# Row group 2 of the products on two banks in turn, the spread on the banks left idle, and bias matmuls with operands stored in pass order

## The chip, the cores and the metric

The kernel runs on one core of a Trainium2 chip. The metric is the device time of one execution in microseconds (us). The kernel before was timed three times, with a median of 274.6 us (274.46 to 275.27). One more execution was profiled, and all rows come from that one. The engines are called by the profile's names: PE is the matrix engine and PEld its weight loads, DVE the vector engine, ACT the activation engine, POOL the general engine, SP the one that issues most transfers.

## The reference, cut to what matters

```
r_goods (2048, 200, 32) fp32, r_candidate_ad (2048, 32) fp32
outer  = einsum('bi,bnj->bnij', candidate_ad, goods).reshape(B, N, 32*32)
h1     = concatenate((broadcast candidate_ad, goods, outer), axis=-1)
act    = sigmoid(h1 @ W1 + b1)          # W1: (32*34, 36), 36 hidden columns
weight = act @ W2 + b2
out    = sum(goods * weight, axis=1)    # (2048, 32)
```

For one batch row the outer product with the candidate can be folded into the weights, so that the first layer is a 32 by 36 matrix of its own for every batch row, and a bias that depends on the candidate.

## The kernel before

**Units and pairs.** A unit is 4 batch rows (one for each group r of 32 partitions), and 8 units make what the code calls a pair p; there are 64 pairs. A set-up stage makes the folded weights of all batch rows: `step` runs fp32 matmuls of 512 columns (line 295), ACT and DVE move them to `wm` and `wxd` (lines 481 and 525), two groups of bias matmuls follow (line 308 into `x_ps`, line 315 into `w_ps`), DVE copies the first four pairs' weights to `wm_ring` (line 537), and the first products start.

**One slot of PE.** In slot p PE executes, in this order, which is written out by hand: half 0 of the products of pair p (line 342, s = 0: for r in 0 to 3 and c in 0 to 3 one 32 by 32 matmul of 200 columns; the trace shows two weight loads and two matmuls for each), the spread of pair p-3, f = 0 (line 426, four bf16 matmuls of 64 by 128), half 1 of the products (s = 1), the spread f = 1, the row sums of pair p-1 (line 387, 12 matmuls of 128 by 32 into `w_ps`), and the x products of pair p (line 363, 8 matmuls of 128 by 32 into `x_ps`, the four hidden columns over 32). The first four slots (`FILL`) are unrolled and the rest is a loop of ten turns of six slots. In slots 0 to 2 there is no spread.

**The other engines.** For a pair, ACT makes eight activates of 200 columns (line 502, r = 0 to 3, s = 0 and 1), one for x (line 508) and one copy to the weight ring (line 489). Its activate of r needs `z_done` of r, which the last matmul of r in half 1 raises. After the second activate of r = 2 it raises `z_read`. DVE then pools: `pool_units` multiplies the spread row sums with the goods and adds them up, 8 instructions a pair, each with a read of the accumulator behind it (line 556), and `keep` takes the row sums out of `w_ps` (lines 544 and 546). POOL splits these into three bf16 parts (lines 263, 265 and 271), which the spread three slots later sums again. SP issues the goods of pair p, four transfers of 200 KB, during slot p-3.

**Banks.** There are eight PSUM banks: `z_ps` 0 to 3, `x_ps`, `w_ps`, `s_ps[0]`, `s_ps[1]`. Products r = 0, 1, 2 always write `z_ps` 0, 1, 2, and r = 3 writes `z_ps` 3 and `s_ps[0]` in turn. The spread writes `w_ps` and `s_ps[1]` (f = 0), and `x_ps` and the bank that r = 3 of the pair before used (f = 1).

**Waits of PE around the change.** Before half 0: `goods_loaded`, `z_read` of the pair before (line 336) and `pooled[1][1]` (line 339). Before the spread f = 0: `w_kept`, `pooled[0][1]` (line 401) and `stack_made`; f = 1: `actx_done`. Before the row sums: `pooled[0][0]`. Before the x products: `pooled[1][0]` (line 359, in every third slot with `wx_laid` besides). `pooled[f][s]` is raised by DVE after the second instruction on bank s of spread f.
Of the kernel before, what the change touches and what calls it, by code (L numbers as in the profile page):

```python
# [7 lines left out]
ALU = mybir.AluOpType  # L8
ACT = mybir.ActivationFunctionType

P = 128
# [36 lines left out]

def build(nc, goods_t, cand_r, cand_u, w1_outer, small, pick, out_t):
    with ExitStack() as ctx:  # L50
# [6 lines left out]
        def sem(name):  # L57
            return ctx.enter_context(nc.semaphore(name))
# [22 lines left out]
        early = act[:, :, :, :].rearrange("p a r n -> p (a r n)")  # L81
        cand = early[:, 0:4 * UNITS].rearrange("p (r u) -> p r u", r=4)
        candu = early[:, 4 * UNITS:5 * UNITS]
        w1 = early[:, 5 * UNITS:5 * UNITS + (T_MAIN + 1) * K].rearrange("p (t j) -> p t j", j=K)
# [20 lines left out]
        def z_bank(p, r):  # L105

            return z_ps[:, r, :] if r < 3 else (z_ps[:, 3, :], s_ps[0][:, :])[p % 2]

        def s_banks(q, f):

            if q + LAG >= PAIRS:

                z0, z1, z2, z3 = (z_ps[:, r, :] for r in range(4))
                return (((z0, z1), (z2, z3)), ((s_ps[1], x_ps), (z0, z1)), ((z2, z3), (s_ps[1], x_ps)))[q + LAG - PAIRS][f]

            return ((w_ps, s_ps[1]), (x_ps, z_bank(q + LAG - 1, 3)))[f]

# [24 lines left out]
        cand_loaded = sem("cand_loaded")  # L143
        candu_loaded = sem("candu_loaded")
        w1_loaded = sem("w1_loaded")
        pick_loaded = sem("pick_loaded")
# [11 lines left out]
        x_done = sem("x_done")  # L158
        z_read = sem("z_read")
        actx_done = sem("actx_done")  # L160
        w_done = sem("w_done")
# [26 lines left out]
        def _(sp):  # L188
            sp.dma_start(cand[:, :, :], cand_r[:, :, :]).then_inc(cand_loaded, 16)

            sp.wait_ge(cand_loaded, 16)
            sp.dma_start(candu[:, :], cand_u[:, :]).then_inc(candu_loaded, 16)
            sp.dma_start(pick_sb[:, :, :], pick[:, :, :]).then_inc(pick_loaded, 16)
            sp.wait_ge(w1_loaded, 16)
            sp.wait_ge(consts_loaded, 16)
            def in_iteration(i, j):

                if j == 0:
                    sp.wait_ge(actx_done, i)
                if j == 1:  # L200
                    sp.wait_ge(z_done, 4 * i + 1)
                if j == 2:
                    sp.wait_ge(z_done, 4 * i + 4)
                if j == 3:
                    sp.wait_ge(z_read, i + 1)

# [75 lines left out]
        def _(pe):  # L282
# [21 lines left out]
            pe.wait_ge(wb_kept[1], kept(T_MAIN - 1, 1))  # L304
            pe.wait_ge(consts_loaded, 16)
            for c in range(4):
                src = cand[0:K, :, :].rearrange("i r (p s c) -> i c r p s", s=2, c=4)
                last = nc.tensor.matmul(x_ps[32 * c:32 * c + 32, :], w1c[0:K, :], src[:, c],  # L308
                                        start=True, stop=True)
            last.then_inc(bias_made, 1)  # L310
            pe.wait_ge(candu_loaded, 16)
            for s in range(2):
                for c in range(4):
                    src = candu[:, :].rearrange("i (p s c) -> i s c p", s=2, c=4)
                    last = nc.tensor.matmul(w_ps[32 * c:32 * c + 32, 0:PAIRS], w1x[:, s, :], src[:, s, c],
                                            start=s == 0, stop=s == 1)
# [7 lines left out]
            def products(p, slot, s, loaded=None):  # L324

                pe.wait_ge(pick_loaded, 16)
                if s == 0:

                    pe.wait_ge(goods_loaded[slot % G_SLOTS], loaded)  # L330
                    if slot < FILL:
                        pe.wait_ge(ring_filled, slot + 1)
                    if slot >= 1:

                        pe.wait_ge(z_read, p)
                    if slot >= LAG + 1:

                        pe.wait_ge(pooled[1][1], p)
                for r in range(4):  # L340
                    for c in range(4):
                        last = nc.tensor.matmul(z_bank(slot, r)[32 * c:32 * c + 32, N * s:N * s + N],  # L342
                                                wm_ring[32 * r:32 * r + 32, slot % RING, 4 * s + c, :],
                                                goods[32 * r:32 * r + 32, slot % G_SLOTS, 4 * s + c, :],
                                                start=True, stop=True)
                    if s == 1:
                        last.then_inc(z_done, 1)
# [43 lines left out]
            def spread(p, slot, f):  # L391

                q = slot - LAG
                if f == 0:
                    pe.wait_ge(stack_made, p)
                    if slot < PAIRS:

                        pe.wait_ge(w_kept, p)
                    if 1 <= q and slot < PAIRS:

                        pe.wait_ge(pooled[0][1], p)
                    if slot == PAIRS:

                        pe.wait_ge(z_read, p)
                    if slot == PAIRS + 1:

                        pe.wait_ge(pooled[0][1], p - 1)
                    if slot == PAIRS + 2:
# [3 lines left out]
                else:  # L412
# [3 lines left out]
                    if slot == PAIRS:  # L416

                        pe.wait_ge(pooled[1][1], p)
                    if slot > PAIRS:
# [48 lines left out]
        def _(sc):  # L468
# [26 lines left out]
            for p in range(PAIRS):  # L495
# [3 lines left out]
                for r in range(4):  # L499
                    sc.wait_ge(z_done, 4 * p + r + 1)  # L500
                    for s in range(2):
                        last = nc.scalar.activation(act[:, p % A_SLOTS, r, N * s:N * s + N],  # L502
                                                    z_bank(p, r)[:, N * s:N * s + N], ACT.Sigmoid,
                                                    bias=bias[:, r, p, s:s + 1])
                    if r == 2:
                        last.then_inc(z_read, 1)
                sc.wait_ge(x_done, p + 1)
# [7 lines left out]
        def _(dve):  # L515
# [31 lines left out]

            def pool_units(q, f, amid=None):
                dve.wait_ge(s_done, 2 * q + f + 1)
                for s in range(2):  # L550
                    if s == 1 and amid is not None:
                        keep(amid)
                    for i in range(2):
                        v = 4 * s + 2 * f + i
                        u = PAIR_U * q + v
                        last = nc.vector.tensor_tensor_reduce(  # L556
                            goods[:, q % G_SLOTS, v, :], s_banks(q, f)[s][:, N * i:N * i + N], goods[:, q % G_SLOTS, v, :],
                            1.0, 0.0, ALU.mult, ALU.add, out_stage[:, u:u + 1])

                    last.then_inc(pooled[f][s], POOLED_FROM[f][s] + 1 if q == 0 else 1)  # L560

            for p in range(PAIRS + LAG):
                q = p - LAG
                if q >= 0:
                    pool_units(q, 0)

                    pool_units(q, 1, PAIRS - 1 if p == PAIRS else None)
                if 1 <= p < PAIRS:
                    keep(p - 1)
# [64 lines left out]
```

## Time and profile before

| what | value |
|---|---|
| three timed runs | 274.46, 274.60, 275.27 us (median 274.6) |
| the profiled execution | 274.75 us, of which the span is 273.0 us |
| mean granted clock of PE | 0.992 of full speed |
| PE, PEld | busy 95% and 47% of the span |
| DVE, ACT, POOL | busy 76%, 82%, 54% |
| chain that ended last | PE 89%, ACT 3%, DVE 3% |
| read from HBM | 54.19 MB, 199 GB/s over the span |

The span runs from the first to the last instruction in the trace; the 1.75 us around it belong to the execution but to none of its instructions. The busy share of PE counts a matmul until the end that the profile models for it, and matmuls overlap, so 95% doesn't mean that nothing more fits. In a timeline, a row gives start and length of a group of like instructions that follow each other; in brackets is the idle time of the engine before it and what ended it.

### The profile page before, as it was taken

How to read it: one execution, taken by the hardware profiler on the slowest of the kernel's cores; microseconds unless marked ns; L12 is line 12 of the kernel's file. 1: busy time of each engine (PE TensorE's matmuls, PEld its weight loads, DVE VectorE, ACT ScalarE, POOL GpSimd, SP SyncE). 2: the span in 40 equal slices, each digit the busy share in tenths (PEclk: the TensorE clock that was granted, in tenths of full speed). 3: DMA queues.
4: the chain of work that ended last, by engine and by line, in shares of the span. 5: the costliest groups of instructions: out<-in, count | busy, mean ns of one | idle time of the engine just before them, and what ended most of it. 6: DMA issues, size and time to landing. Idle time of an engine off the chain costs nothing.

```text
span 273.0 us, 18351 instructions
## 1 busy us (share of the span) xinstructions
PE 258.4 (95%) x7492; PEld 127.4 (47%) x7492; DVE 208.0 (76%) x1176; ACT 223.2 (82%) x658; POOL 146.7 (54%) x285
## 2 busy tenths in 40 slices
PE   8997999999999999999999999999999999999980
PEld 2324544444454544555445554454544445445540
DVE  0892567877778777787777877778777787777886
ACT  2998878888898888988889888898888988889850
POOL 1300664565555755557555575555665556655562
PEclk9999999999999999999999999999999999999996
DMA  5872766767776777776787777777777776776100
GB/s 200 254 289 62 224 208 186 226 210 232 223 214 213 215 227 228 217 208 204 229 232 214 216 206 226 224 223 214 202 221 233 217 208 206 231 235 209 39 1 10
DMA packets 38195, 54.84 MB, mean 201 GB/s; under 512 B 4240, under 2 KB 37904, under 8 KB 38032
## 3 DMA queue, kind: packets, MB, share of 16 engines
q1 hardware_dynamic: 37872, 54.15, 66.3%
q10 hardware_dynamic: 288, 0.32, 0.3%
q8 instruction: 11, 0.18, 0.3%
q14 instruction: 24, 0.20, 0.2%
HBM read 54.19 MB, written 0.26 MB: 199 GB/s over the span
## 4 chain that ended last, share of the span: by engine, by line
PE 89%; ACT 3%; DVE 3%; DMA 2%; issue 2%; DVEq 0%
PE z_ps L342 27%; PE w_ps L387 25%; PE x_ps L363 18%; PE w_ps L426 6%; PE x_ps L426 6%; ACT act L502 3%; PE z_ps L295 3%; DVE goods L556 2%; DMA act<-w_outer 2%; PE s_ps L342 1%; PE s_ps L295 1%; PE x_ps L295 1%; PE x_ps L308 1%; PE w_ps L295 0%; PE s_ps L426 0%
## 5 line engine op out<-in xcount | busy, mean ns | idle before, releaser
L502 ACT ACTIVATE act<-z_ps,bias 128x200 f32<-128x200 f32 x448 | 149.4, 439 | 34.2 <-PE z_ps L342 17.7
L342 PE MATMUL z_ps<-goods,wm_ring 32*32 32x200 f32 x3584 | 79.6, 339 | 5.7 <-ACT act L502 1.9
L556 DVE CUSTOM_DVE_ANT_0 goods<-w_ps,goods 128x200 f32<-128x200 f32 x122 | 39.8, 364 | 45.2 <-PE s_ps L426 45.2
L263 POOL TENSOR_TENSOR rest<-whole,top 128x200 f32<-128x200 f32 x64 | 36.1, 565 | 66.7 <-DVE top L546 36.7
L556 DVE CUSTOM_DVE_ANT_0 goods<-s_ps,goods 128x200 f32<-128x200 f32 x186 | 60.1, 361 | 0.0
L363 PE MATMUL x_ps<-goods,wx 128*32 128x200 f32 x1024 | 56.7, 338 | 0.2
L387 PE MATMUL w_ps<-act,consts 128*32 128x200 f32 x1024 | 56.6, 339 | 0.3 <-ACT actx L508 0.3
L265 POOL TENSOR_SCALAR mid<-rest,consts 128x200 bf16<-128x200 f32 x64 | 50.1, 783 | 6.3
L342 PEld LDWEIGHTS z_ps<-goods,wm_ring 32*32 32x32 f32 x3584 | 32.1, 103 | 39.3 <-issue 38.6
L241 POOL COPY wx<-wxd 32x96 f32<-32x96 f32 (+1 forms) x88 | 22.9, 260 | 42.3 <-PE x_ps L363 28.1
L556 DVE DVE_READ_ACCUMULATOR2_ANT out_stage<- 128x1 f32 x512 | 42.5, 83 | 0.0
L556 DVE CUSTOM_DVE_ANT_0 goods<-x_ps,goods 128x200 f32<-128x200 f32 x126 | 40.8, 361 | 0.0
L363 PEld LDWEIGHTS x_ps<-goods,wx 128*32 128x32 f32 x1024 | 28.6, 109 | 24.6 <-DVE out_stage L556 12.3
L271 POOL TENSOR_TENSOR stack<-rest,mid 128x200 bf16<-128x200 f32 x64 | 36.3, 567 | 5.4
L342 PE MATMUL s_ps<-goods,wm_ring 32*32 32x200 f32 x512 | 34.7, 340 | 0.0
L387 PEld LDWEIGHTS w_ps<-act,consts 128*32 128x32 f32 x1024 | 26.8, 109 | 16.1 <-DVE out_stage L556 10.0
L387 PE MATMUL w_ps<-actx,consts 128*32 128x200 f32 x512 | 33.4, 333 | 0.0
L544 DVE TENSOR_SCALAR whole<-w_ps,consts 128x200 f32<-128x200 f32 x64 | 27.0, 422 | 7.6 <-PE w_ps L387 7.6
L426 PE MATMUL s_ps<-stack,pick_sb 64*128 64x200 bf16 x186 | 31.9, 252 | 0.5 <-POOL stack L271 0.5
L508 ACT ACTIVATE actx<-x_ps,biasx 128x200 f32<-128x200 f32 x64 | 30.6, 478 | 0.0
L489 ACT ACTIVATE wm_ring<-wm 128x256 f32<-128x256 f32 x60 | 28.9, 482 | 0.0
L502 ACT ACTIVATE act<-s_ps,bias 128x200 f32<-128x200 f32 x64 | 24.9, 466 | 0.0
(45 smaller groups left out, 225.5 us busy)
## 6 DMA issues: line engine op xcount, KB each, us to landing
goods<-goods_t SPq DMA_DIRECT2D x256, 200.0 KB, 2.8
act<-cand_r SPq DMA_DIRECT2D x1, 1024.0 KB, 5.3
act<-cand_u SPq DMA_DIRECT2D x1, 256.0 KB, 2.7
out_t<-out_stage SPq DMA_DIRECT2D x4, 64.0 KB, 2.6
consts<-small ACTq DMA_DIRECT2D x1, 164.5 KB, 5.3
act<-w_outer ACTq DMA_DIRECT2D x1, 144.0 KB, 5.5
pick_sb<-pick SPq DMA_DIRECT2D x1, 128.0 KB, 2.6
```

The costliest lines, as they stand in the source:

```text
L263: nc.gpsimd.tensor_tensor(rest[:, :], whole[:, q % 2, :], top[:, q % 2, :], ALU.subtract).then_inc(part_step, 1)
L265: nc.gpsimd.tensor_scalar(mid[:, :], rest[:, :], m2, None, ALU.mult).then_inc(part_step, 1)
L271: nc.gpsimd.tensor_tensor(stack[:, q % 2, :], rest[:, :], mid[:, :], ALU.subtract).then_inc(stack_made, STACK_FROM + 1 if q == 0 else 1)
L342: last = nc.tensor.matmul(z_bank(slot, r)[32 * c:32 * c + 32, N * s:N * s + N], wm_ring[32 * r:32 * r + 32, slot % RING, 4 * s + c, :], go ...
L363: last = nc.tensor.matmul(x_ps[32 * c:32 * c + 32, 0:N], left, goods[:, slot % G_SLOTS, 4 * s + c, :], start=s == 0, stop=s == 1)
L387: last = nc.tensor.matmul(w_ps[32 * t:32 * t + 32, 0:N], left, right, start=step == 0, stop=step == 2)
L426: last = nc.tensor.matmul(s_banks(q, f)[s][:, N * i:N * i + N], pick_sb[rows, 2 * f + i, :], stack[rows, q % 2, :], start=True, stop=True)
L489: nc.scalar.activation(*of_ring(p), ACT.Identity)
L502: last = nc.scalar.activation(act[:, p % A_SLOTS, r, N * s:N * s + N], z_bank(p, r)[:, N * s:N * s + N], ACT.Sigmoid, bias=bias[:, r, p, s ...
L508: nc.scalar.activation(actx[:, p % A_SLOTS, :], x_ps[:, 0:N], ACT.Sigmoid, bias=biasx[:, p:p + 1]).then_inc(actx_done, 1)
L544: nc.vector.tensor_scalar(whole[:, p % 2, :], w_ps[:, 0:N], b2, None, ALU.add).then_inc(w_kept, KEPT_FROM + 1 if p == 0 else 1)
L556: last = nc.vector.tensor_tensor_reduce(goods[:, q % G_SLOTS, v, :], s_banks(q, f)[s][:, N * i:N * i + N], goods[:, q % G_SLOTS, v, :], 1. ...
```

## The change

Row group 2 of the products now alternates as row group 3 does: r = 2 writes `z_ps` 2 or `s_ps[0]`, r = 3 writes `z_ps` 3 or `s_ps[1]`. The spread f = 0 writes `w_ps` and the bank that r = 2 of the pair before used, f = 1 writes `x_ps` and that of r = 3. ACT raises `z_read` after r = 1 and a new `z2_read` after r = 2; half 0 waits for the first, the spread f = 0 for the second. The wait for `pooled[1][1]` moves from before half 0 to between r = 1 and r = 2 of half 0, and `pooled[0][1]` moves there from the spread. DVE pools in another order: the second unit of f = 0 on the z bank comes after the two units of `x_ps`, so that `x_ps` is free after five units instead of six. In the set-up the operands of the bias matmuls come from a new array `candb` (its own transfer on SP's queue, between those of `candu` and `pick_sb`) and a reordered `candu`, so that PE reads neighbouring elements. The order of PE's matmuls and their number stay.

```
 def z_bank(p, r):
-    return z_ps[:, r, :] if r < 3 else (z_ps[:, 3, :], s_ps[0][:, :])[p % 2]
+    return z_ps[:, r, :] if r < 2 or p % 2 == 0 else s_ps[r - 2][:, :]
 def s_banks(q, f):
     if q + LAG >= PAIRS:
         z0, z1, z2, z3 = (z_ps[:, r, :] for r in range(4))
-        return (((z0, z1), (z2, z3)), ((s_ps[1], x_ps), (z0, z1)), ((z2, z3), (s_ps[1], x_ps)))[q + LAG - PAIRS][f]
-    return ((w_ps, s_ps[1]), (x_ps, z_bank(q + LAG - 1, 3)))[f]
+        return (((z0, z1), (z2, z3)), ((s_ps[0], s_ps[1]), (z0, z1)), ((z2, z3), (s_ps[0], s_ps[1])))[q + LAG - PAIRS][f]
+    return ((w_ps, x_ps)[f], z_bank(q + LAG - 1, 2 + f))
...
 @block.sync
             sp.dma_start(candu[:, :], cand_u[:, :]).then_inc(candu_loaded, 16)
+            sp.dma_start(candb[:, :, :], cand_b[:, :, :]).then_inc(candb_loaded, 16)
             sp.dma_start(pick_sb[:, :, :], pick[:, :, :]).then_inc(pick_loaded, 16)
...
                 if j == 3:
-                    sp.wait_ge(z_read, i + 1)
+                    sp.wait_ge(z2_read, i + 1)
...
+            pe.wait_ge(candb_loaded, 16)
             for c in range(4):
-                src = cand[0:K, :, :].rearrange("i r (p s c) -> i c r p s", s=2, c=4)
-                last = nc.tensor.matmul(x_ps[32 * c:32 * c + 32, :], w1c[0:K, :], src[:, c],
+                last = nc.tensor.matmul(x_ps[32 * c:32 * c + 32, :], w1c[0:K, :], candb[:, c, :],
...
-                    src = candu[:, :].rearrange("i (p s c) -> i s c p", s=2, c=4)
+                    src = candu[:, :].rearrange("i (s c p) -> i s c p", s=2, c=4)
...
 def products(p, slot, s, loaded=None):
                         pe.wait_ge(z_read, p)
-                    if slot >= LAG + 1:
+                for r in range(4):
+                    if s == 0 and r == 2 and slot >= LAG + 1:
+                        pe.wait_ge(pick_loaded, 16)
+                        pe.wait_ge(pooled[0][1], p)
                         pe.wait_ge(pooled[1][1], p)
-                for r in range(4):
                     for c in range(4):
...
 def spread(p, slot, f):
                         pe.wait_ge(w_kept, p)
-                    if 1 <= q and slot < PAIRS:
-                        pe.wait_ge(pooled[0][1], p)
+                        pe.wait_ge(z2_read, p)
...
                     if slot == PAIRS:
+                        pe.wait_ge(pooled[0][1], p)
                         pe.wait_ge(pooled[1][1], p)
...
 @block.scalar
+                    if r == 1:
+                        last.then_inc(z_read, 1)
                     if r == 2:
-                        last.then_inc(z_read, 1)
+                        last.then_inc(z2_read, 1)
...
 @block.vector
-                    pool_units(q, 0)
-                    pool_units(q, 1, PAIRS - 1 if p == PAIRS else None)
+                    dve.wait_ge(s_done, 2 * q + 1)
+                    pool_unit(q, 0, 0, 0)
+                    pool_unit(q, 0, 0, 1)
+                    pool_unit(q, 0, 1, 0)
+                    if p >= PAIRS:
+                        pool_unit(q, 0, 1, 1)
+                    dve.wait_ge(s_done, 2 * q + 2)
+                    pool_unit(q, 1, 0, 0)
+                    pool_unit(q, 1, 0, 1)
+                    if p < PAIRS:
+                        pool_unit(q, 0, 1, 1)
+                    if p == PAIRS:
+                        keep(PAIRS - 1)
+                    pool_unit(q, 1, 1, 0)
+                    pool_unit(q, 1, 1, 1)
```

`pool_unit(q, f, s, i)` is the body of the old inner loop, one instruction; it raises `pooled[f][s]` where i is 1.

## Rows read from the trace of the kernel before

**Rows 1.** The page: busy time by engine (part 1), and transfers (part 6).
```profile
PE 258.4 (95%) x7492; PEld 127.4 (47%) x7492; DVE 208.0 (76%) x1176; ACT 223.2 (82%) x658; POOL 146.7 (54%) x285
...
goods<-goods_t SPq DMA_DIRECT2D x256, 200.0 KB, 2.8
```

**Rows 2.** Timeline of PE's weight loads, one slot: start, length, line, groups.
```profile
145.34 0.22 PEld L342 LDWEIGHTS z_ps<-goods,wm_ring 32*32 32x32 f32 x21 [0.44 <-issue]
...
145.93 0.09 PEld L426 LDWEIGHTS w_ps<-stack,pick_sb 64*128 64x128 bf16 x1 [0.32 <-issue]
...
146.21 0.18 PEld L342 LDWEIGHTS z_ps<-goods,wm_ring 32*32 32x32 f32 x20 [0.16 <-issue]
...
146.76 0.09 PEld L426 LDWEIGHTS x_ps<-stack,pick_sb 64*128 64x128 bf16 x1 [0.32 <-issue]
...
147.04 0.50 PEld L387 LDWEIGHTS w_ps<-act,consts 128*32 128x32 f32 x16 [0.16 <-DVE out_stage L556]
...
149.12 0.29 PEld L342 LDWEIGHTS z_ps<-goods,wm_ring 32*32 32x32 f32 x23 [0.35 <-issue]
```

**Rows 3.** Timeline of PE's matmuls, the same slot.
```profile
145.46 0.37 PE L342 MATMUL s_ps<-goods,wm_ring 32*32 32x200 f32 x4
...
146.03 0.25 PE L426 MATMUL s_ps<-stack,pick_sb 64*128 64x200 bf16 x1
...
146.48 0.35 PE L342 MATMUL s_ps<-goods,wm_ring 32*32 32x200 f32 x4
...
148.28 0.89 PE L363 MATMUL x_ps<-goods,wx 128*32 128x200 f32 x16
```

**Rows 4.** Timeline of ACT: the slot before, and this one.
```profile
143.10 2.65 ACT L502 ACTIVATE act<-z_ps,bias 128x200 f32<-128x200 f32 x8 [0.49 <-PE z_ps L342]
...
145.90 0.48 ACT L489 ACTIVATE wm_ring<-wm 128x256 f32<-128x256 f32 x1
146.88 2.01 ACT L502 ACTIVATE act<-z_ps,bias 128x200 f32<-128x200 f32 x6 [0.49 <-PE s_ps L342]
```

**Rows 5.** Timeline of DVE, the same slot.
```profile
146.32 0.37 DVE L556 CUSTOM_DVE_ANT_0 goods<-w_ps,goods 128x200 f32<-128x200 f32 x1 [0.70 <-PE s_ps L426]
...
148.04 0.08 DVE L556 DVE_READ_ACCUMULATOR2_ANT out_stage<- 128x1 f32 x1
...
148.62 0.08 DVE L556 DVE_READ_ACCUMULATOR2_ANT out_stage<- 128x1 f32 x1
```

**Rows 6.** Source view of line 339, 148.5 to 149.3: duration ns, first and last start.
```profile
L339 PEldq EVENT_SEMAPHORE  x1: 51/51/51, 149.0 to 149.0; - x1
```

**Rows 7.** Weight loads and matmuls of slot 1, and starts of slots 3, 63.
```profile
23.73 0.22 PEld L342 LDWEIGHTS z_ps<-goods,wm_ring 32*32 32x32 f32 x21 [1.62 <-issue]
...
24.99 0.50 PEld L387 LDWEIGHTS w_ps<-act,consts 128*32 128x32 f32 x16 [0.32 <-issue]
...
25.87 0.64 PEld L363 LDWEIGHTS x_ps<-goods,wx 128*32 128x32 f32 x16
...
26.03 0.86 PE L363 MATMUL x_ps<-goods,wx 128*32 128x200 f32 x16
...
30.33 0.22 PEld L342 LDWEIGHTS z_ps<-goods,wm_ring 32*32 32x32 f32 x21 [0.52 <-issue]
...
259.12 0.22 PEld L342 LDWEIGHTS z_ps<-goods,wm_ring 32*32 32x32 f32 x21 [0.44 <-issue]
```

**Rows 8.** Source view of line 332 (a wait behind slot 1's x products), 25 to 26.
```profile
L332 PEldq EVENT_SEMAPHORE  x1: 51/51/51, 25.7 to 25.7; - x1
```

**Rows 9.** The set-up: groups by line (busy us, mean ns), then two timeline rows.
```profile
L295 PE MATMUL z_ps<-act 32*32 32x512 f32 x160 | 9.2, 600 | 0.1
...
L308 PE MATMUL x_ps<-act,consts 32*32 32x512 f32 x8 | 2.0, 1066 | 0.0
...
19.67 0.50 DVE L537 COPY wm_ring<-wm 128x256 f32<-128x256 f32 x2
...
20.37 0.93 PEld L342 LDWEIGHTS z_ps<-goods,wm_ring 32*32 32x32 f32 x64 [0.21 <-issue]
```

More of the change, by code:

```diff
@@ L46, with build @@
 C_ALL = C_M2 + 1
-def build(nc, goods_t, cand_r, cand_u, w1_outer, small, pick, out_t):
+def build(nc, goods_t, cand_r, cand_b, cand_u, w1_outer, small, pick, out_t):
     with ExitStack() as ctx:
@@ L82, in build @@
         cand = early[:, 0:4 * UNITS].rearrange("p (r u) -> p r u", r=4)
+        candb = sb("candb", [K, 4, 4 * 2 * PAIRS])
         candu = early[:, 4 * UNITS:5 * UNITS]
@@ L144, in build @@
         candu_loaded = sem("candu_loaded")
+        candb_loaded = sem("candb_loaded")
         w1_loaded = sem("w1_loaded")
@@ L159, in build @@
         z_read = sem("z_read")
+        z2_read = sem("z2_read")
         actx_done = sem("actx_done")
@@ L398, in spread @@
                         pe.wait_ge(w_kept, p)
-                    if 1 <= q and slot < PAIRS:
-                        pe.wait_ge(pooled[0][1], p)
+                        pe.wait_ge(z2_read, p)
                     if slot == PAIRS:
                         pe.wait_ge(z_read, p)
-                    if slot == PAIRS + 1:
-                        pe.wait_ge(pooled[0][1], p - 1)
                     if slot == PAIRS + 2:
@@ L546, in keep, with pool_unit @@
                 nc.vector.tensor_scalar(top[:, p % 2, :], whole[:, p % 2, :], m1, None, ALU.mult).then_inc(top_made, 1)
[L548 to L560, printed above, removed]
+            def pool_unit(q, f, s, i):
+                v = 4 * s + 2 * f + i
+                u = PAIR_U * q + v
+                one = nc.vector.tensor_tensor_reduce(
+                    goods[:, q % G_SLOTS, v, :], s_banks(q, f)[s][:, N * i:N * i + N], goods[:, q % G_SLOTS, v, :],
+                    1.0, 0.0, ALU.mult, ALU.add, out_stage[:, u:u + 1])
+                if i == 1:
+                    one.then_inc(pooled[f][s], POOLED_FROM[f][s] + 1 if q == 0 else 1)
             for p in range(PAIRS + LAG):
@@ L586 @@
     by_unit = np.asarray(r_candidate_ad).reshape(UNITS, 4, K).transpose(1, 2, 0)
-    cand_u = np.ascontiguousarray(by_unit).reshape(P, UNITS)
+    by_pair = by_unit.reshape(4, K, PAIRS, 2, 4)
+    cand_u = np.ascontiguousarray(by_pair.transpose(0, 1, 3, 4, 2)).reshape(P, UNITS)
+    cand_b = np.ascontiguousarray(by_pair.transpose(1, 4, 0, 2, 3)).reshape(K, 4, 4 * 2 * PAIRS)
     cand_r = np.ascontiguousarray(np.tile(by_unit.transpose(1, 0, 2), (4, 1, 1)))
@@ L624 @@
     arrays, args = {}, []
-    for name, a in (("goods_t", goods_t), ("cand_r", cand_r), ("cand_u", cand_u), ("w1_outer", w1_outer),
+    for name, a in (("goods_t", goods_t), ("cand_r", cand_r), ("cand_b", cand_b), ("cand_u", cand_u), ("w1_outer", w1_outer),
                     ("small", small), ("pick", pick.reshape(P, 4, P))):
```

## The prediction, made before the changed kernel was run

> **What bounds the kernel now.** I read the page first. PE is busy 95% of the span, ACT 82%, DVE 76% [rows 1], and the chain of waits runs through PE nearly all the way. That says only that PE has hardly any empty moment, not that its work sets the pace, since a matmul counts until its modelled end. So I went to the timelines of one slot in mid-loop and asked, for each start on PE, what it could have started at.
>
> The slot runs from 145.34 to 149.12, a period of 3.78 us [rows 2]. Inside it each change of tile form starts its first weight load 0.07 before the modelled end of the last matmul ahead of it: the spread's matmul ends at 146.28 and half 1 loads at 146.21; the last group of half 1 ends at 146.83 and the spread loads at 146.76 [rows 2, 3]. I take this 0.07 as the mark of a start that waits for PE alone. At the end of the slot the mark is missed, though barely: the x products end at 148.28 + 0.89 = 149.17 and the next half 0 loads at 149.12. More telling is slot 1, where nothing makes the x products wait: they load 0.88 after the row sums' first load (24.99, 25.87) and end 1.90 after it (26.89) [rows 7]. With the mark, the next half 0 could load 1.90 - 0.07 = 1.83 after the row sums' first load. In the loop it is 149.12 - 147.04 = 2.08 [rows 2]. So 0.25 us of each slot is not PE's work.
>
> Two waits share it. The first is a closed loop with ACT. Half 0 loads at 145.34, ACT's first activate starts at 146.88 (1.54 later), its sixth, the second of r = 2, ends at 148.89 (2.01 later) [rows 4], and half 0 of the next slot loads at 149.12 (0.23 later, in which PE's sequencer executes two waits; the second, of 51 ns, starts at 149.0, about 0.1 ahead of the load [rows 2, 6]). 1.54 + 2.01 + 0.23 = 3.78, the whole period, so this loop sets the pace. The second is DVE: the sixth accumulator read, which frees `x_ps`, ends at 148.12 [rows 5], against a load that PE could make at 147.04 + 0.88 = 147.92. Removing only one of the two would leave most of the time where it is.
>
> **The change, part by part.** *z_read after r = 1.* The activates start 0.31 apart (eight take 2.65, the last 0.47 of it) [rows 4], so the signal comes 0.62 earlier and the loop needs 1.54 + 1.39 + 0.23 = 3.16 us. It no longer binds.
>
> *DVE's order.* `x_ps` is free after the fifth unit. Units are 0.29 apart (148.62 - 148.04 for two), so it ends at 148.12 - 0.29 = 147.83 [rows 5]. A signal takes some 0.04 (DVE starts at 146.32 behind the spread's end at 146.28 [rows 3, 5]); with 0.06 for signal and load I get 147.89, in time for 147.92. Where a second wait stands before it, in every third slot, it is some 0.04 late, but in slot 1 the matmul starts 0.16 behind its load (26.03 against 25.87) [rows 7], which covers that. The fourth unit now needs the spread f = 1, which ends at 147.04 + 0.07 = 147.11, so DVE could start it at 147.15; its turn comes at 146.32 + 3 x 0.29 = 147.19. No stall, with 0.04 to spare.
>
> Here a rule of the Trainium skill speaks against the gain. The page "TensorE: Matmul & The Clock Gate", section "Part 3: Packing small matmuls — row/col tiling", says that a weight load overlaps matmuls in flight only if it is for another row group. Loads of x and row sums use all rows, so by it an early signal would buy nothing. Slot 1 shows the x loads beginning at 25.87 while row-sum matmuls are in flight, so I go by the row and keep the rule as a rival.
>
> *The wait inside half 0.* This is what the change adds, and the trace of before has no such wait. Behind it in PE's order stand the loads of r = 2 and 3, and behind these the spread and everything else. The semaphores themselves are early: the eighth read ends at 148.70, about 148.74 at PE, and half 0 would start at 145.34 + 3.54 = 148.88 at the earliest. What remains is the sequencer's time. Below: nothing, if it executes the wait ahead of the array. It can do so, since the wait behind slot 1's x products starts at 25.7 and the first of these loads at 25.87 [rows 7, 8]. Above: the whole 0.23 from signal to load. r = 3 starts its matmuls 0.12 after half 0's first load [rows 2, 3], so r = 2 starts near 0.05; if the wait is executed only with the first loads, r = 2 comes near 0.10. I take 0.05. In exchange half 0 loses one of the two waits ahead of it. Half 0 lasts 0.59 and half 1, which has no wait of its own, 0.55 [rows 2], so the new half 0 is 0.55 + 0.05 = 0.60 (0.55 to 0.78).
>
> *z2_read before the spread f = 0.* It comes at 148.89, needed at 148.88 + 0.60. Hidden by half 0, 0.55 to spare.
>
> *The sum for a slot.* Half 0 0.60, spread 0.28, half 1 0.55, spread 0.28 [rows 2], row sums to the next load 1.83: 3.54 instead of 3.78, 0.24 less.
>
> *Who else must keep up.* ACT's ten instructions take 143.10 to 146.38, 3.28 [rows 4]; DVE is busy 76% of the time, 2.9 of a slot, and POOL 54% [rows 1]. All are under 3.54. Goods are issued three slots ahead and land in 2.8 us [rows 1], against 10.6. DVE's new order delays the second of a pair's four transfers by two units, 0.58, and the two behind it on SP's queue follow; three slots hide that.
>
> *Set-up.* Reading 512 neighbouring columns takes 600 ns a matmul and the strided bias matmuls 1066 [rows 9]; the second set of four starts behind the first, so some 0.9 us go. The path gets less, since DVE's copy to the ring is next: of two that take 0.50 together the first starts at 19.67 and ends, by my estimate, at 19.96, and with 0.12 for signal, wait and load the products start at 20.08 instead of 20.37 [rows 9]. 0.29 less. The new transfer is 64 KB beside goods of 200 KB each. Its issue stands ahead of the goods on SP's queue; slot 0 waits for the ring copy, so I take nothing for it.
>
> *Slots 0 to 3.* The wait of 1.62 before slot 1 [rows 7] is on z_read: 0.62 less. Slots 1 and 2 have no spread and need 24.99 - 23.73 + 1.83 = 3.09 each; now they take (30.33 - 23.73) / 2 = 3.30. 0.42 less. But the row sums of slot 1 then wait for ACT's x activate, by my estimate 0.27: that activate moves up by 0.29 only, PE by 0.91. Together 0.62 + 0.42 - 0.27 + 0.29 = 1.06.
>
> *Total.* From slot 3 (30.33) to slot 63 (259.12) there are 60 periods [rows 7], and slot 63 itself: 61 x 0.24 = 14.6. With 1.06 it is 15.7. The tail behind, DVE's, keeps its order and its length. The profiled execution took 274.75, so 259.05; the median of the runs is 0.15 lower. I say 259.0 us.
>
> **The rivals.** *The sequencer can't look past the wait* (row groups 2 and 3 start 0.2 late, half 0 0.75, period 3.69): 61 x 0.09 + 1.06 = 6.6, so 268. For it: two waits and a load do cost 0.23 today. Against: rows 8.
>
> *The x products gain nothing from DVE's order*, the skill's rule above, as a mechanism here: they load at 148.12 + 0.06 = 148.18, 1.14 after the row sums, and take 0.89, so the next half 0 loads 1.96 after these instead of 1.83. The period is 3.67, 61 x 0.11 + 1.06 = 7.8, so 267. Slot 1 speaks against it.
>
> *Another loop holds the slot near 3.78*, for instance goods that come late, and the change does nothing in the loop: only 1.06 goes, 273.7. No row has PE waiting for goods.
>
> *Slower*: the wait empties the array, and r = 2 and 3 run behind r = 0 and 1 in full. A half's matmul row has 0.35 to 0.37 [rows 3], about 0.33 of it new time, so half 0 becomes 0.93 and the period 3.87: 61 x 0.09 - 1.06 = 4.4 more, 279. It decides from a half 0 above 0.86, that is when the wait costs over 0.3.
>
> **How the numbers follow.** Forecast 0.68, sequencer 0.13, x products 0.08, nothing in the loop 0.05, slower 0.04, the rest 0.02 unnamed. A measurement of this kernel tells 0.3%, 0.8 us, from no change. Faster by more: 0.68 + 0.13 + 0.08 and most of the 0.05 (273.7 is just past the bound), 0.92; the same 0.03; slower 0.05. The forecast's own range is a period of 3.50 to 3.60, 256.9 to 262.7. The range given reaches to the x products' case and to the sequencer's, whose cost isn't known: 257 to 268.5.
>
> **What would show it.** Period 3.54; half 0 about 0.60 and r = 2's matmuls 0.10 behind its start; every change of tile form, that into half 0 too, 0.07 before the end ahead of it; x loads 0.88 behind the row sums; ACT idle some 0.25 a slot. The first products near 20.1, slot 3 near 29.3. I am wrong if half 0 is long, or if x still follows DVE at 1.14.

## The result, and the profile after

The changed kernel takes 262.6 us, the median of four runs (262.55 to 263.06). The kernel before, run in turn with it, took 274.9 us (274.46 to 275.62). The ratio is 0.9554, with a 95% interval of 0.9528 to 0.9579: 4.5% faster. The forecast was 259.0 us with a range of 257.0 to 268.5. The direction and the route were right, and 3.5 us of the forecast gain of 15.7 did not come. The profiled execution took 262.6 us with a span of 260.8, against 273.0 before: 12.2 us less.

The page of the changed kernel: busy time by engine, the x products' loads with the idle time ahead of them, and the new transfer (KB, us from issue to landing).

```profile
PE 248.3 (95%) x7492; PEld 133.6 (51%) x7492; DVE 209.6 (80%) x1176; ACT 224.3 (86%) x658; POOL 147.0 (56%) x285
...
L370 PEld LDWEIGHTS x_ps<-goods,wx 128*32 128x32 f32 x1024 | 33.0, 109 | 10.6 <-issue 0.3
...
candb<-cand_b SPq DMA_DIRECT2D x1, 256.0 KB, 3.8
```

PE is busy 95% before and after [rows 1], though the span is 12.2 us shorter: its busy time fell by 10.1 us with the same 7492 matmuls, since more of them overlap. So the share doesn't tell the room that is left. The x products now load with 10.6 us of idle time ahead of 1024 loads, and what ended most of it is no longer DVE. The transfer for `candb` is 256 KB. The prediction called it 64 KB; it hides either way, since the loads of the bias matmuls wait 0.4 us for ACT's `wm` in both kernels and not for it.

The timeline of PE's weight loads in one slot, which answers to [rows 2]: start, length, groups.

```profile
139.75 0.18 PEld L349 LDWEIGHTS z_ps<-goods,wm_ring 32*32 32x32 f32 x16 [0.32 <-issue]
139.85 0.21 PEld L349 LDWEIGHTS s_ps<-goods,wm_ring 32*32 32x32 f32 x16
140.38 0.09 PEld L430 LDWEIGHTS w_ps<-stack,pick_sb 64*128 64x128 bf16 x1 [0.32 <-issue]
...
140.66 0.15 PEld L349 LDWEIGHTS z_ps<-goods,wm_ring 32*32 32x32 f32 x12 [0.16 <-issue]
...
141.21 0.09 PEld L430 LDWEIGHTS x_ps<-stack,pick_sb 64*128 64x128 bf16 x1 [0.32 <-issue]
...
141.49 0.50 PEld L394 LDWEIGHTS w_ps<-act,consts 128*32 128x32 f32 x16 [0.16 <-DVE out_stage L557]
...
142.41 0.59 PEld L370 LDWEIGHTS x_ps<-goods,wx 128*32 128x32 f32 x16
143.33 0.31 PEld L349 LDWEIGHTS z_ps<-goods,wm_ring 32*32 32x32 f32 x32 [0.32 <-issue]
```

The slot lasts 143.33 - 139.75 = 3.58 (3.572 is the median over the loop from slot 16 on), where 3.54 was forecast. Half 0 takes 0.63, the spread 0.28, half 1 0.55, the spread 0.28, and the row sums to the next load 1.84. PE's matmuls in the same slot (timeline):

```profile
142.19 0.52 PE L394 MATMUL w_ps<-actx,consts 128*32 128x200 f32 x8
142.53 0.87 PE L370 MATMUL x_ps<-goods,wx 128*32 128x200 f32 x16
```

The x products end at 142.53 + 0.87 = 143.40, and the next half 0 loads at 143.33, 0.07 ahead: the mark of a start that waits for PE alone is now met at the end of the slot too. ACT, in the timeline of the same slot, has slack where it had set the pace:

```profile
141.33 1.38 ACT L506 ACTIVATE act<-z_ps,bias 128x200 f32<-128x200 f32 x4 [0.27 <-PE s_ps L349]
```

Its idle time was forecast at some 0.25 a slot.

**Where the time went.** I took the start of half 0 in every slot of both profiled executions and split the span at four of them. The rows of after that carry this (PE's weight loads; the rows of before are in [rows 7], except slot 10, which started at 58.12):

```profile
20.12 1.04 PEld L349 LDWEIGHTS z_ps<-goods,wm_ring 32*32 32x32 f32 x64 [0.88 <-ACT wm L485]
...
29.30 0.15 PEld L349 LDWEIGHTS z_ps<-goods,wm_ring 32*32 32x32 f32 x12 [0.32 <-issue]
...
57.56 0.24 PEld L349 LDWEIGHTS z_ps<-goods,wm_ring 32*32 32x32 f32 x20 [0.32 <-issue]
...
246.93 0.18 PEld L349 LDWEIGHTS z_ps<-goods,wm_ring 32*32 32x32 f32 x16 [0.32 <-issue]
```

| stretch | before | after | gained | forecast |
|---|---|---|---|---|
| start to slot 3 | 30.33 | 29.30 | 1.03 | 1.06 |
| slots 3 to 10 (7 slots, the loop's first turn and a slot) | 27.79 | 28.26 | -0.47 | 7 x 0.24 = 1.7 |
| slots 10 to 63 (53 slots) | 201.00 | 189.37 | 11.63 | 53 x 0.24 = 12.7 |
| slot 63 to the end | 13.84 | 13.88 | -0.04 | 0.24 |
| span | 273.0 | 260.8 | 12.2 | 15.7 |

So 3.5 us are short, and the largest part, 2.2, is in seven slots at the beginning. The prediction had no line for them. That 2.2 is one execution against one: the changed kernel profiled again (e11 below) took 28.95 for the seven, which would make it 2.8.

### The profile page after: what moved, and what is told of

It is laid out like the page before. It is cut to its first block, busy times and chain, and to the rows that moved or that the text cites. A ratio compares the mean times of both kernels' runs of the same rounds, so it can differ in the third digit from the quotient of the medians.

```text
span 260.8 us, 18353 instructions
## 1 busy us (share of the span) xinstructions
PE 248.3 (95%) x7492; PEld 133.6 (51%) x7492; DVE 209.6 (80%) x1176; ACT 224.3 (86%) x658; POOL 147.0 (56%) x285
## 4 chain that ended last, share of the span: by engine, by line
PE 87%; ACT 7%; DVE 2%; DMA 2%; issue 1%; ACTq 0%; DVEq 0%
PE w_ps L394 28%; PE z_ps L349 25%; PE x_ps L370 16%; PE w_ps L430 6%; PE x_ps L430 6%; PE s_ps L349 4%; ACT wm L485 4%; DMA act<-w_outer 2%; DVE goods L557 2%; ACT act L506 2%; ACT wxd L485 1%; PE z_ps L300 0%; ACT actx L514 0%; DVE whole L550 0%; PE z_ps L430 0%
## 5 line engine op out<-in xcount | busy, mean ns | idle before, releaser
L506 ACT ACTIVATE act<-z_ps,bias 128x200 f32<-128x200 f32 x384 | 129.4, 440 | 20.5 <-PE z_ps L349 10.9
L370 PE MATMUL x_ps<-goods,wx 128*32 128x200 f32 x1024 | 55.4, 333 | 0.0
L349 PEld LDWEIGHTS z_ps<-goods,wm_ring 32*32 32x32 f32 x3072 | 30.3, 103 | 34.4 <-issue 33.0
L557 DVE CUSTOM_DVE_ANT_0 goods<-z_ps,goods 128x200 f32<-128x200 f32 x140 | 44.9, 361 | 0.0
L506 ACT ACTIVATE act<-s_ps,bias 128x200 f32<-128x200 f32 x128 | 44.9, 461 | 0.0
L557 DVE CUSTOM_DVE_ANT_0 goods<-s_ps,goods 128x200 f32<-128x200 f32 x128 | 41.3, 361 | 0.0
L557 DVE CUSTOM_DVE_ANT_0 goods<-x_ps,goods 128x200 f32<-128x200 f32 x122 | 39.5, 361 | 1.3 <-PE s_ps L430 1.0
L370 PEld LDWEIGHTS x_ps<-goods,wx 128*32 128x32 f32 x1024 | 33.0, 109 | 10.6 <-issue 0.3
L349 PE MATMUL s_ps<-goods,wm_ring 32*32 32x200 f32 x1024 | 37.0, 339 | 0.0
```

Of the source, the lines that this page charges most:

```text
L370: last = nc.tensor.matmul(x_ps[32 * c:32 * c + 32, 0:N], left, goods[:, slot % G_SLOTS, 4 * s + c, :], start=s == 0, stop=s == 1)
L557: one = nc.vector.tensor_tensor_reduce(goods[:, q % G_SLOTS, v, :], s_banks(q, f)[s][:, N * i:N * i + N], goods[:, q % G_SLOTS, v, :], 1.0 ...
```

## Experiments

The question was twofold: which of the two waits carried the gain, and where the missing 3.5 us are. All times stand beside runs of the kernel before on the same chip, whose medians were 274.8 to 275.1 us. The line numbers in a row are those of the kernel it comes from.

### The banks without DVE's order, DVE's order without the banks

**e1**: the changed kernel with DVE's order of units as it was.

```diff
...
-                    pool_unit(q, 0, 1, 0)
...
-                    dve.wait_ge(s_done, 2 * q + 2)
-                    pool_unit(q, 1, 0, 0)
-                    pool_unit(q, 1, 0, 1)
-                    if p < PAIRS:
-                        pool_unit(q, 0, 1, 1)
...
+                    pool_units(q, 0)
+                    pool_units(q, 1, PAIRS - 1 if p == PAIRS else None)
```

> The changed kernel with DVE's old order of units, so that x_ps is free after the sixth unit again. If the x products follow DVE as before, they load about 1.14 us after the row sums in two slots of three and 1.2 in the third, the slot becomes 3.70 to 3.79 us (mean near 3.73) instead of 3.57, and the time rises by some 8 to 9 us, to 271. If DVE's order was worth nothing (weight loads that use the same row groups can't overlap the row sums anyway), the slot stays at 3.57 and the time at 262.6.

Measured: 271.2 us (270.2 to 271.5), ratio 0.9866 [0.9846, 0.9886]. PE's weight loads in one slot of it:

```profile
140.62 0.50 PEld L394 LDWEIGHTS w_ps<-act,consts 128*32 128x32 f32 x16 [0.16 <-DVE out_stage L562]
...
141.77 0.50 PEld L370 LDWEIGHTS x_ps<-goods,wx 128*32 128x32 f32 x16 [0.31 <-DVE out_stage L562]
142.59 0.18 PEld L349 LDWEIGHTS z_ps<-goods,wm_ring 32*32 32x32 f32 x16 [0.32 <-issue]
```

The x products load 1.15 behind the row sums and wait for DVE. The next half 0 follows 1.97 behind the row sums, as the second rival had worked out (1.96). Its slot is 3.70 with half 0 at 0.63, and 3.79 in every third slot, where two waits stand ahead of the x products: 3.73 in the mean.

**e2**: the kernel before, with only DVE's new order.

```diff
-                    pool_units(q, 0)
-                    pool_units(q, 1, PAIRS - 1 if p == PAIRS else None)
...
+                    pool_unit(q, 0, 1, 0)
...
+                    dve.wait_ge(s_done, 2 * q + 2)
+                    pool_unit(q, 1, 0, 0)
+                    pool_unit(q, 1, 0, 1)
+                    if p < PAIRS:
+                        pool_unit(q, 0, 1, 1)
...
```

> The kernel before with DVE's new order alone. If the loop over ACT (products, activates up to r = 2, z_read, products) sets the pace, the slot stays at 3.78 us and the time at 274.9, though the x products now load 0.88 us behind the row sums. If PE's work from the row sums on was the pace, the slot falls by about 0.12 and the time to 267.

Measured: 275.2 us (274.2 to 276.0), ratio 1.0002 [0.9984, 1.0020]. PE's weight loads:

```profile
139.98 0.50 PEld L387 LDWEIGHTS w_ps<-act,consts 128*32 128x32 f32 x16 [0.16 <-DVE out_stage L551]
...
140.85 0.64 PEld L363 LDWEIGHTS x_ps<-goods,wx 128*32 128x32 f32 x16
142.06 0.27 PEld L342 LDWEIGHTS z_ps<-goods,wm_ring 32*32 32x32 f32 x32 [0.56 <-issue]
```

The x products load 0.87 behind the row sums, as forecast, and nothing comes of it. The idle time ahead of half 0 grows to 0.56 from 0.35 in [rows 2], and the slot stays at 3.78. The stall only moved, to the wait for `z_read`. Together the two runs show what the prediction had read from the timelines. The loop with ACT set the pace, DVE's order was the next bound, and each alone hides the other. DVE's order by itself is worth nothing, the rest of the change without it 274.9 - 271.2 = 3.7 us, and both together 12. The 3.7 are not the banks alone. e1 keeps the new set-up, the earlier slot 1 and the wait inside half 0; its slot 3 starts at 29.38, 0.95 sooner than before, and its slots 10 to 63 take 3.73 against 3.79.

### The set-up alone

**e3**: the kernel before, with `candb` and the reordered `candu`.

```diff
+            sp.dma_start(candb[:, :, :], cand_b[:, :, :]).then_inc(candb_loaded, 16)
...
-                last = nc.tensor.matmul(x_ps[32 * c:32 * c + 32, :], w1c[0:K, :], src[:, c],
+                last = nc.tensor.matmul(x_ps[32 * c:32 * c + 32, :], w1c[0:K, :], candb[:, c, :],
```

> The kernel before with the set-up's part alone: the bias matmuls read candb and the reordered candu. The bias matmuls take about 0.9 us less, but the first products wait for DVE's copy to the ring next, so they start 0.25 us sooner (20.1 instead of 20.4) and the time falls by 0.25 to 0.3 us, to 274.6. If nothing else stood behind them, it would fall by 0.9.

Measured: 274.3 us (273.9 to 275.5), ratio 0.9981 [0.9963, 0.9999]. The bias matmuls in the view by line (busy us, mean ns), and DVE's copy to the ring and the first products' loads in the timeline:

```profile
L311 PE MATMUL x_ps<-candb,consts 32*32 32x512 f32 x8 | 1.1, 600 | 0.0
```

```profile
20.05 0.50 DVE L540 COPY wm_ring<-wm 128x256 f32<-128x256 f32 x2
...
20.46 0.49 PEld L345 LDWEIGHTS z_ps<-goods,wm_ring 32*32 32x32 f32 x34 [0.90 <-ACT wm L484]
```

A matmul takes 600 ns in place of 1066, as the other 512-column matmuls do in [rows 9]. Of the time, up to 1 us fits the interval, and so does nearly nothing. In this execution the first products did not even start earlier (20.46 against 20.37), and among the profiled executions of kernels that share this set-up the start lay between 19.94 and 20.52. That spread comes from upstream, since the copy itself started between 19.53 and 20.11. Counted from the copy's start, the first products load 0.41 later here and 0.40 or 0.41 in all ten profiles that share this set-up, against 0.70 before [rows 9] and 0.77 in e2. So the path did get 0.29 shorter, and the copy is what PE waits for now.

### The wait inside half 0

The forecast gave 0.05 to the wait between r = 1 and r = 2. The changed kernel's chain of waits shows it, with the pieces of half 0 first and those of half 1 behind the spread (start, length):

```profile
139.82 0.33 PE z_ps L349 x8
140.15 0.12 PE s_ps L349 x7
140.28 0.05 PE z_ps L349 x7
140.32 0.13 PE s_ps L349 x8
...
140.73 0.33 PE z_ps L349 x8
141.06 0.05 PE s_ps L349 x8
141.11 0.12 PE z_ps L349 x8
```

In half 1 the second piece takes 0.05, in half 0 it takes 0.12: r = 2 and 3 come 0.07 later. The wait is executed only with the half's first loads (source view of its line; half 0 loads at 139.75 and 143.33, and in the trace the wait starts 0.023 behind these):

```profile
L347 PEldq EVENT_SEMAPHORE  x2: 51/51/51, 139.8 to 143.3; - x2
```

**e4**: both waits ahead of half 0, everything else as changed. **e10** is the same kernel again with more rounds, and **e11** the changed kernel again beside it.

```diff
-                for r in range(4):
-                    if s == 0 and r == 2 and slot >= LAG + 1:
-
-                        pe.wait_ge(pick_loaded, 16)
+                    if slot >= LAG + 1:
                         pe.wait_ge(pooled[0][1], p)
                         pe.wait_ge(pooled[1][1], p)
+                for r in range(4):
```

> The changed kernel with both pooled waits before half 0 instead of inside it. If the wait inside costs the 0.075 us by which half 0 (0.63) exceeds half 1 (0.55), half 0 becomes 0.55 to 0.59, the slot 3.50 to 3.54, and the time falls by 2 to 4 us, to 259 or 260.5. If the waits ahead of half 0 now hold it up (pooled[1][1] comes about 0.15 us before PE is free), the slot stays near 3.57 or grows and the time stays at 262.6 or above.

> The version with both pooled waits before half 0 once more, with more rounds, beside the changed kernel on one chip. 260.5, 2 us below the changed kernel, with the slot at 3.51 from slot 10 on and the first turn again held by code loading: slots 3 to 9 in 28 to 29.5 us, about what the slower kernels take for them.

> The changed kernel again, on the chip of the run before it: 262.6, slot 3.57, slots 3 to 9 in 27.5 to 28.5 us.

Measured: e4 260.5 us (260.0 to 261.6), ratio 0.9477 [0.9446, 0.9509]; e10 260.0 us (259.6 to 260.5), ratio 0.9443 [0.9428, 0.9458]; e11 263.2 us (261.8 to 263.9), ratio 0.9555 [0.9529, 0.9580]. The intervals of e10 and e11 don't overlap: the waits ahead of half 0 are 3.1 us better, 1.2%. PE's weight loads in e10:

```profile
142.73 0.25 PEld L347 LDWEIGHTS z_ps<-goods,wm_ring 32*32 32x32 f32 x32 [0.32 <-issue]
143.29 0.09 PEld L428 LDWEIGHTS w_ps<-stack,pick_sb 64*128 64x128 bf16 x1 [0.32 <-issue]
...
146.24 0.15 PEld L347 LDWEIGHTS z_ps<-goods,wm_ring 32*32 32x32 f32 x12 [0.32 <-issue]
```

Half 0 is 0.56 here (0.567 in the loop, against 0.630 in the changed kernel) and the slot 3.51. The wait inside half 0, which the change brings on top of the banks, costs 0.063 a slot and buys next to nothing: ahead of half 0 the two signals are already there in nearly every slot. Six of the 53 slots of e10 from slot 10 on took 3.54 to 3.64, so in the mean the slot is 0.05 shorter.

**e6**: the changed kernel with two more waits at that place, on semaphores met long before. A stand-alone wait instruction holds two semaphores, so this is one more instruction of the sequencer.

```diff
                     if s == 0 and r == 2 and slot >= LAG + 1:
                         pe.wait_ge(pick_loaded, 16)
+                        pe.wait_ge(candb_loaded, 16)
+                        pe.wait_ge(candu_loaded, 16)
                         pe.wait_ge(pooled[0][1], p)
```

> The changed kernel with two more waits inside half 0, on transfers that landed long ago, which make one more instruction for PE's sequencer. If what half 0 lost is sequencer time, each such instruction costs about 0.1 us there: half 0 0.73, slot 3.67, time 268 to 269. If the sequencer runs ahead of the array, nothing changes: 262.6.

Measured: 268.4 us (267.8 to 269.5), ratio 0.9766 [0.9732, 0.9799]. PE's weight loads, and then the source view of the two wait instructions:

```profile
141.91 0.18 PEld L351 LDWEIGHTS z_ps<-goods,wm_ring 32*32 32x32 f32 x16 [0.32 <-issue]
142.12 0.21 PEld L351 LDWEIGHTS s_ps<-goods,wm_ring 32*32 32x32 f32 x16
142.65 0.09 PEld L432 LDWEIGHTS w_ps<-stack,pick_sb 64*128 64x128 bf16 x1 [0.32 <-issue]
```

```profile
L348 PEldq EVENT_SEMAPHORE  x2: 51/51/51, 141.9 to 145.6; - x2
...
L349 PEldq EVENT_SEMAPHORE  x2: 51/51/51, 142.0 to 145.7; - x2
```

Row groups 2 and 3 now load 0.21 behind the start, against 0.10 in the changed kernel. Half 0 is 0.74 and the slot 3.685. So it is the instruction that costs, not the signal. The first costs 0.063 (half 0 0.567 without, 0.630 with), of which, as I read it, a part lies beside the loads of r = 0 and 1 (that part was not tried by itself). The next costs 0.11 (3.685 - 3.572), all of it on the path; the two instructions start 0.11 apart in the trace.

### The first turn of PE's loop

The seven slots from 3 on, one by one (from start of half 0 to the next):

| slot | 3 | 4 | 5 | 6 | 7 | 8 | 9 |
|---|---|---|---|---|---|---|---|
| before | 3.78 | 3.78 | 4.73 | 4.18 | 3.78 | 3.78 | 3.78 |
| changed | 3.51 | 3.85 | 4.66 | 3.96 | 3.58 | 4.71 | 3.99 |

Before, slots 5 and 6 were long. They still are, and 8 and 9 are long now too. The chain of waits of the changed kernel in slot 5:

```profile
36.73 0.49 PE z_ps L349 x14
37.23 0.53 issue
37.75 0.35 PE z_ps L349
```

PE stops in the middle of a half, between two products that wait for no engine. One suspect is the loading of its own code, since the loop's instructions are all new in its first turn. The transfers view has a queue of kind "instruction", q8, that moves 16 KB pieces. In the changed kernel it is there from 29.3 to 57.6 and gone from 58 to 246:

```profile
q8 instruction: 7, 0.11, 1.9%
```

**e7**: the first turn unrolled and the loop left with nine turns. The instructions executed stay the same, but six slots more run on code of their own.

```diff
+FLAT = FILL + RING
...
-            for p in range(FILL):
-                products(p, p, 0, 64)
+            for p in range(FLAT):
+                products(p, p, 0, 64 * (1 + p // G_SLOTS))
...
-            with pe.Fori(0, TURNS):
+            with pe.Fori(0, TURNS - 1):
```

> The changed kernel with one turn of PE's loop (six slots) written out ahead of the loop, which runs nine turns; the work is the same. If the slots of the first turn are held by the loading of PE's code (mean 4.1 us instead of 3.57 over slots 4 to 9), six more slots pay it: 2 to 3 us more, 265, with irregular slots up to slot 16. If something of the start of the kernel holds them (the goods' first transfers), the time stays at 262.6 and the slots are regular from slot 10.

Measured: 267.1 us (264.2 to 267.7), ratio 0.9675 [0.9614, 0.9736], 4.5 us more than the changed kernel. The four runs differ more than usual, and the profiled one is the slowest, so the figures of its slots are at the upper end. Slots 10 to 15, regular at 3.57 in the changed kernel, took 4.03, 6.02, 3.81, 3.63, 4.09 and 4.25, which is 25.8 for six, and from slot 16 on they are regular. The transfers view from 58 to 83, then the chain of waits in the worst of these slots:

```profile
q8 instruction: 5, 0.08, 1.2%
```

```profile
64.36 0.32 PE x_ps L371 x2
64.68 1.94 issue
66.62 0.88 PE x_ps L371 x14
```

The breaks go where the new code goes, and so do q8's transfers, the last of them near 82 us. So PE stops where code is new, whatever the slot's number.

That q8's transfers are what it waits for can be read from the times of its pieces. In the changed kernel the piece before the stop of slot 5 ended at 36.22, and PE went on at 37.75. The piece before the stop of slot 8 ended at 49.59, and PE went on at 50.97. In e7 the piece ended at 65.06 and PE went on at 66.62. From slot 3 to slot 63 the twelve profiles have 30 such stops inside a group (more than 0.4 us between two matmul starts of one line). Each of the 30 ends 1.27 to 1.62 us after the end of a piece. They come at the same few places in PE's order in every kernel: near its 850th, 975th, 1225th and 1350th matmul, and in e7 also near the 1606th and the 1981st. A piece took 0.88 to 1.95 us. So a stop is a piece that came too late for PE.

A table of the slots 3 to 10 over all kernels whose goods are whole in that stretch says what that does to a gain (e9 is described below; there the stretch is that of the changed kernel):

| kernel | regular slot | slots 3 to 10 | over 7 regular slots |
|---|---|---|---|
| before | 3.78 | 27.79 | 1.3 |
| e2 | 3.78 | 28.12 | 1.6 |
| e3 | 3.78 | 28.11 | 1.7 |
| e1 | 3.73 | 27.46 | 1.4 |
| e6 | 3.685 | 27.84 | 2.0 |
| changed, e11, e9 | 3.572 | 28.26, 28.95, 29.51 | 3.3, 3.9, 4.5 |
| e7 | 3.573 | 27.74 | 2.7 |
| e4, e10 | 3.51 | 29.19, 29.11 | 4.6, 4.5 |

The stretch takes 27.5 to 29.5 us whatever the slot would be, and the same kernel varies in it by 1.25 from one execution to the next. A shorter slot has gained nothing there.

**e8** asked whether the goods' traffic delays the code: the changed kernel with a quarter of the goods loaded for pairs 7 to 15. **e9** is its control, the same for pairs 27 to 35.

```diff
-                    sp.dma_start(goods[:, p % G_SLOTS, v:v + 2, :].rearrange("p u n -> p (u n)"),
...
+                    rows = slice(0, 32) if 7 <= p < 16 else slice(0, P)
+                    sp.dma_start(goods[rows, p % G_SLOTS, v:v + 2, :].rearrange("p u n -> p (u n)"),
...
```

> The changed kernel with the goods of pairs 7 to 15 brought for 32 of the 128 partitions only, so part of the products and sums of these pairs is made from older goods; PE's instructions and waits are the same. Their transfers run during slots 4 to 12. If the code transfers of the first turn are late because they share the transfer engines with the goods, slots 3 to 9 fall from 28.3 us to near 7 x 3.57 = 25.0 and the time by 2 to 3 us, to 260. If the code comes late by itself (asked for too late, whatever else runs), the time stays near 262.6.

> The control of the run before it: the same cut for pairs 27 to 35, whose transfers run after the first turn, when no code of the loop is loaded. If only the first turn suffers from the goods' traffic, nothing changes: 262.6. If goods' traffic slows PE anywhere, the slots 24 to 32 become shorter than 3.57 and the time falls as in the other run.

Measured: e8 261.3 us (260.3 to 262.7), ratio 0.9480 [0.9458, 0.9502]; e9 262.7 us (262.0 to 264.3), ratio 0.9529 [0.9510, 0.9548], with slots 24 to 32 at 3.57 as in the changed kernel. So by the timed runs the traffic of the first turn is worth something: e8 is 1.4 us below its control, and their intervals just don't touch (the changed kernel beside them, e11, is 1.9 above e8). The control shows that goods play no part in a slot whose code is there.

How the traffic does it, the one profile of e8 doesn't show. Its execution was the slowest of the four (262.7, the others 260.3 to 261.6). Slots 7 to 9 took 3.57 each, where the changed kernel had 3.58, 4.71 and 3.99: the later breaks are gone. But the seven slots together took 28.43, no less than the changed kernel's 28.26, because slot 5 took 6.8 instead of 4.7. PE's weight loads of slot 5 in e8, and then the load behind the same stop in the changed kernel:

```profile
36.37 0.17 PEld L350 LDWEIGHTS z_ps<-goods,wm_ring 32*32 32x32 f32 x14 [0.32 <-issue]
38.02 0.13 PEld L350 LDWEIGHTS z_ps<-goods,wm_ring 32*32 32x32 f32 x2 [1.47 <-issue]
```

```profile
37.75 0.13 PEld L349 LDWEIGHTS z_ps<-goods,wm_ring 32*32 32x32 f32 x2 [0.92 <-issue]
```

The windows view (length, busy time and count of PE, PEld, DVE, ACT and POOL, granted clock as a share of 2.4 GHz, DMA share, GB/s) over slot 5 of e8, and over slot 5 and half of slot 6 of the changed kernel:

```profile
36.40:43.20 6.80, 5.72 (x124) 2.87 (x124) 3.60 (x20) 3.93 (x13) 1.92 (x3) 0.76 0.27 58
```

```profile
36.70:43.20 6.50, 5.97 (x186) 2.91 (x184) 4.04 (x23) 4.55 (x14) 3.21 (x6) 1.00 0.70 195
```

The stop was longer, 1.47 against 0.92, and from 39.91 to 43.32 the granted clock was 0.5, the 1.2 GHz level. With both in it, slot 5 is 2.1 us longer. The pieces of q8 didn't come faster with less traffic: the six from slot 4 to slot 9 took 0.95 to 1.72 us, against 0.90 to 1.76 in the changed kernel. So a rival stands beside "less traffic removes the later breaks": PE was 2 us late after slot 5, and the loader had that much time to get ahead. No run separates the two. What set the length of the stop in slot 5 stays open as well.

One version was not measured: a single semaphore inside half 0, carried by the weight load itself. So whether any wait costs there, or only one with an instruction of its own, stays open.

## Why the prediction came out as it did

The measured 262.6 lies just inside the forecast's own 256.9 to 262.7, which it gave for a period of 3.50 to 3.60. (The lower end is a slip: 61 x 0.28 + 1.06 = 18.1 off 274.75 is 256.6.) The period came out inside too, 3.572, but the sum with 3.572 would be 261.0. So the mechanism of the slot held, and the edge of the range was reached by two things that the sum lacks, the first turn and the tail.

**What bounds the kernel.** Right. Two waits shared 0.25 of a slot, ACT's loop first and DVE next. e2 shows ACT's loop standing alone, e1 DVE's order.

**z_read after r = 1.** Right: ACT idles 0.27 a slot, and half 0 meets the mark of 0.07.

**DVE's order.** Right, within 0.04: x loads 0.87 to 0.92 behind the row sums, where 0.88 was forecast. The rival that drew on the Trainium skill ("TensorE: Matmul & The Clock Gate", "Part 3: Packing small matmuls — row/col tiling") falls. In the changed kernel the x loads, on all 128 rows, begin at 142.41, and the row sums' last matmuls end at 142.19 + 0.52 = 142.71. The modelled end stands 0.30 behind the first load here, and 0.30 to 0.35 in the slots from 16 on. The measurement decides against the sentence that only another row group lets a load overlap. The same section of the Trainium skill also names loads into a background weight buffer as pulled ahead; which of its cases this is, no run here tells.

**The wait inside half 0.** This term was mis-sized. The prediction named both ends and took 0.05, which gave half 0 0.60. It measured 0.630: 0.063 for the wait (e10 against the changed kernel), on a half that without a wait lasts 0.567, not 0.55. The wait was not executed ahead of the array as in [rows 8]; it came with the first loads. Over the 53 slots from 10 to 63 the 0.032 between 3.572 and 3.54 makes 1.7 us. Part of it was made up elsewhere: these slots took 3.79 each before and not 3.78, so the stretch is short by 1.1 only.

**The first turn of the loop.** This is the step that failed. "From slot 3 (30.33) to slot 63 (259.12) there are 60 periods" gave 0.24 to each, though [rows 7] with the period of [rows 2] already held the warning. (259.12 - 30.33) / 60 is 3.813, not 3.78: 2.0 us of the stretch were not periods, and 1.3 of them lay in the first turn. There PE runs on code that is new (e7) and stops until a piece of it has come (the times of q8's pieces), so a faster slot only reaches the next piece sooner. Of 1.7 forecast, -0.5 came: 2.2 us, the largest part of the 3.5.

**The tail.** It was given one more 0.24, for slot 63, and got nothing. The weight loads of the spread and of the last row sums in the changed kernel:

```profile
250.50 0.28 PEld L430 LDWEIGHTS z_ps<-stack,pick_sb 64*128 64x128 bf16 x8 [0.32 <-issue]
...
251.53 0.50 PEld L394 LDWEIGHTS w_ps<-act,consts 128*32 128x32 f32 x16 [0.75 <-ACT actx L514]
```

The row sums load 1.03 behind the spread, against 0.81 before (263.68 - 262.87), because PE has come further ahead of ACT and waits for its last x activate. What the slot gave, this wait took back.

**Set-up and first slots.** 1.03 came of 1.06 by slot 3, and term by term. The first products start 0.25 earlier (forecast 0.29; the copy to the ring started 0.04 later in this execution, and from it the gain is the full 0.29). Slot 0 is 0.62 shorter (0.62), slots 1 and 2 together 0.16 (0.42 - 0.27 = 0.15).

**The rivals.** The other loop, the x products' case and the slower case did not happen. The sequencer's case was half right: the wait is not looked past, but it costs 0.063 and not 0.20. I take it that the loads of r = 0 and 1 run beside it, since a second instruction there costs 0.11.

## What to carry to other kernels

When two waits end close together, undo them in a table of pairs: here the change without DVE's order was worth 3.7 us, DVE's order alone nothing, and both 12. Don't put a stand-alone wait between the small matmuls of a short group, even on a signal long met: put it ahead of the group, where the sequencer's 0.1 us lies beside the work before. And don't multiply a gain per slot by all slots: divide the whole stretch by its count first, and where that is more than the regular slot (3.813 against 3.78), look for the slots in which something else, such as code that comes for the first time, sets the time.

## What the runs showed of the hardware

- A wait instruction of 51 ns inside a group of 32 by 32 matmuls cost 0.063 us for the first and 0.11 for the next, with its semaphores met. Ahead of the group, behind other matmuls, the waits left a regular slot at 3.51, though six of 53 slots took up to 3.64.
- In its first pass over the loop's code PE stopped inside groups, for 0.53 and 0.62 us in the changed kernel and 1.94 in e7, while 16 KB pieces came on a queue of their own. All 30 such stops in the twelve profiles end 1.27 to 1.62 us after the end of a piece. Six unrolled slots cost 25.8 - 6 x 3.57 = 4.4 us.
- After a stop of 1.47 us in e8 (36.55 to 38.02) PE worked on, and from 39.91 to 43.32 the granted clock was 0.5. In all other profiles it was 1.0 in that stretch. The longer stop in e7 (2.33 in the same view) had no such fall behind it.
- An fp32 matmul of 512 columns took 600 ns from neighbouring elements and 1066 ns from every fourth element, 16 bytes apart.
